# Two changes to a one-core MoE + LoRA kernel: VectorE's rows without a loop, and a later place for an adding transfer

## The reference, cut to what matters

```python
# x (8, 512, 256), cond_8 (8, 8); all float32
rw = softmax(cond_8); w, sel = top_k(rw, 2); w = w / w.sum(-1)      # two experts per batch row
mlp(x, g, u, d) = (gelu(x @ g) * (x @ u)) @ d                        # 256 -> 1024 -> 256
y  = x + mlp(x, shared) + sum over the two experts e of w[b, e] * mlp(x, skill e)
lora(y) = sum over e of cond_8[b, e] * (y @ As[e].T) @ Bs[e].T
out = y + y @ W_base.T + b_base + 2 * lora(y)
```

## Time and profile before

| | |
|---|---|
| runs | 799.68, 799.92, 800.48 us; median 799.92 |
| profiled execution | 800.2 us, of which the span from the first to the last instruction is 798.5 us |
| PE | 790.7 us busy (99%), 4277 matmuls, granted clock 1.000 |
| DVE | 653.6 us busy (82%), 874 instructions |
| ACT | 497.6 us busy (62%) |
| POOL | 311.5 us busy (39%) |
| HBM | 83.53 MB read, 24.64 MB written |

### The profile page before, as it was taken

How to read it: one execution, slowest core, us unless ns; L and a number is a source line. 1 busy time by engine, 2 the same in 40 slices (tenths; PEclk the granted TensorE clock), 3 DMA queues, 4 the chain that set the end, 5 groups by cost and what they waited for, 6 DMA issues and landing times.

```text
span 798.5 us, 14174 instructions
## 1 busy us (share of the span) xinstructions
PE 790.7 (99%) x4277; PEld 687.0 (86%) x4277; DVE 653.6 (82%) x874; ACT 497.6 (62%) x808; POOL 311.5 (39%) x308
## 2 busy tenths in 40 slices
PE   9999999999999999999999999999999999999998
PEld 7888888888888888889889888888998888898897
DVE  4866888888887788878978987888898789789787
ACT  5654564564664576766767666576675667666663
POOL 1531321321430355355344542634634443553441
PEclk9999999999999999999999999999999999999999
DMA  7426506304726742682664465277346526723400
GB/s 202 128 75 197 146 1 195 123 0 145 232 71 185 251 106 77 207 191 81 209 162 110 127 222 123 78 236 173 103 146 206 122 79 219 175 79 107 117 14 28
DMA packets 139894, 108.82 MB, mean 136 GB/s; under 512 B 63040, under 2 KB 131392, under 8 KB 139840
## 3 DMA queue, kind: packets, MB, share of 16 engines
q1 hardware_dynamic: 138688, 104.00, 43.4%
q0 software_dynamic: 1152, 4.19, 3.3%
HBM read 83.53 MB, written 24.64 MB: 135 GB/s over the span
## 4 chain that ended last, share of the span: by engine, by line
PE 89%; issue 4%; POOL 4%; DVE 1%; ACT 1%; POOLq 0%; DVEq 0%; ACTq 0%
PE ps_ring L859 55%; PE ps_acc L859 32%; POOL post L819 1%; POOL stage L805 1%; POOL stage L810 1%; POOL stage L808 1%; POOL stage L806 1%; DVE xc L1589 0%; PE ps_ring L981 0%; PE ps_acc L1075 0%; PE ps_acc L975 0%; DVE wide L1589 0%; PE ps_ring L880 0%; PE ps_ring L885 0%; PE ps_ring L889 0%
## 5 line engine op out<-in xcount | busy, mean ns | idle before, releaser
L859 PE MATMUL ps_ring<-xc,wide 128*128 128x512 f32 (+1 forms) x1854 | 385.6, 356 | 0.0
L859 PEld LDWEIGHTS ps_ring<-xc,wide 128*128 128x128 f32 x1854 | 317.0, 189 | 53.0 <-DVE post L1651 1.0
L1204 ACT CAST inner_hi<-post 128x512 fp32r<-128x512 f32 x192 | 116.2, 621 | 97.6 <-DVE post L1988 32.3
L859 PE MATMUL ps_acc<-inner_hi,wide 128*128 128x512 f32 x504 | 166.4, 390 | 0.0
L1589 DVE TENSOR_TENSOR inner_lo<-post,inner_hi 128x512 fp32r<-128x512 f32 (+1 forms) x145 | 136.4, 950 | 4.0 <-ACT inner_hi L1204 3.7
L1207 ACT ACTIVATE post<-post 128x256 f32<-128x256 f32 (+1 forms) x114 | 62.2, 558 | 99.9 <-DVE post L1912 70.6
L819 POOL TENSOR_TENSOR post<-post 128x256 f32<-128x256 f32 x78 | 82.0, 1071 | 91.4 <-ACT post L1456 91.4
L859 PEld LDWEIGHTS ps_acc<-inner_hi,wide 128*128 128x128 f32 x504 | 94.8, 188 | 18.9
L859 PE MATMUL ps_acc<-inner_lo,wide 128*128 128x512 f32 x252 | 98.5, 391 | 0.0
L859 PE MATMUL ps_acc<-inner_hi,sh_dn 128*128 128x512 f32 x256 | 83.9, 389 | 0.0
L740 POOL TENSOR_TENSOR post<-post 128x512 f32<-128x512 f32 x24 | 31.0, 1293 | 127.3 <-DVE post L1653 127.3
(11 more groups left out here) (127 smaller groups left out, 1067.5 us busy)
## 6 DMA issues: line engine op xcount, KB each, us to landing
rights_scratch<-xc SPq DMA_DIRECT2D x6, 1792.0 KB, 10.2
raw<-n_L_cond_skill_gate_dram SPq DMA_DIRECT2D x32, 256.0 KB, 3.0
raw<-in_L_cond_skill_up_dram SPq DMA_DIRECT2D x32, 256.0 KB, 3.6
raw<-n_L_cond_skill_down_dram SPq DMA_DIRECT2D x32, 256.0 KB, 3.9
xbuf<-n_L_cond_skill_gate_dram SPq DMA_DIRECT2D x32, 256.0 KB, 2.9
xbuf<-in_L_cond_skill_up_dram SPq DMA_DIRECT2D x32, 256.0 KB, 3.4
xbuf<-n_L_cond_skill_down_dram SPq DMA_DIRECT2D x32, 256.0 KB, 3.6
xt_scratch<-xbuf SPq DMA_DIRECT2D x8, 512.0 KB, 3.3
```

Source lines behind the costliest of these rows:

```text
L859: last = pe.matmul(dst, left_[a], right_[b], start=start and n == 0, stop=stop and n == len(PASSES) - 1, skip_group_check=adds)
L1204: return nc.scalar.copy(dst, src)
```

## The change

1. DVE's rows 1 to 7 are called one after another from a Python loop, so the instructions of each are written out and there is no jump; all waits of DVE have constants.
2. On POOL, `add_tokens(b)` moves from behind `ex_c22(b, 1)` to behind `ex_c22(b, 3)` in all rows but the last.
3. In `acc1_to_stage` and `layer1_constants` three waits are dropped, and two pairs of operations on halves become one operation each.

```diff
@@ POOL's row
                 sums_of_weights(b, 2)
                 ex_c22(b, 1)
-                add_tokens(b)
+                if last:
+                    add_tokens(b)
                 sums_of_weights(b, 3)
                 sums_of_weights(b, 4)
                 ex_c22(b, 2)
                 ex_c22(b, 3)
                 if not last:
+                    add_tokens(b)
                     sums_of_weights(b + 1, 0)
                 ex_c22(b, 4)
@@ DVE
             def acc1_to_stage(q):
-                if q > 0:
-                    dve.wait_ge(acc0_out, 2 * q)
                 dve.wait_ge(sh_down_done, 2 * PAIRS * (q + 1))
...
             def layer1_constants():
-
-                dve.wait_ge(acc0_out, 2 * Q)
-                dve.wait_ge(layer1_landed, 6 * 16)
                 dve.wait_ge(a_hi, 1)
-                for half in (slice(0, P), slice(P, H)):
-                    last = take_lo(a_s[1][:, half], a_nat[:, half], a_s[0][:, half])
-                last.then_inc(a_ready, 1)
+                take_lo(a_s[1], a_nat, a_s[0]).then_inc(a_ready, 1)
                 dve.wait_ge(turned_w, 1)
                 V.tensor_copy(b_t[:], ps_misc[1][:, 0:H]).then_inc(b_t_done, 1)
-                for c in range(HC):
-                    last = V.tensor_copy(w_id[:, c * H:(c + 1) * H], ps_misc[0][:, c * H:(c + 1) * H])
-                last.then_inc(w_turned, 1)
+                V.tensor_copy(w_id[:], ps_misc[0][:]).then_inc(w_turned, 1)
...
-            def row(b, par, first, last, steps=range(K)):
+            def row(b, par, first, last):
...
-                for k in steps:
+                for k in range(K):
...
             row(0, 0, True, False)
-            row(1, 1, False, False, range(DVE_TURN_STEP))
-            with dve.Fori(0, (B - 2) // 2) as i:
-                row(i * 2 + 1, 1, False, False, range(DVE_TURN_STEP, K))
-                row(i * 2 + 2, 0, False, False)
-                row(i * 2 + 3, 1, False, False, range(DVE_TURN_STEP))
-            row(B - 1, 1, False, True, range(DVE_TURN_STEP, K))
+            for b in range(1, B):
+                row(b, b % 2, False, b == B - 1)
             dve.wait_ge(base_ready, B * 16)
```

More of the change, by code:

```diff
@@ L64, in cond_resid_kernel @@
     TURN_STEP = 6
-    DVE_TURN_STEP = 8
     SEVEN = [1, 3, 5, 6, 7]
```

## The result

The changed kernel takes 804.97 us (median of 6 runs, 804.46 to 807.30) against 799.80 us before: 1.0067 times as long, 95% interval 1.0054 to 1.008. It is slower where 795.5 us was forecast. The profiled execution was 805.2 us with a span of 803.5.

The account below looks back on a forecast made before the run. PE was taken as the bound, busy 790.7 of 798.5 us, losing time in rows 3 and 5 to DVE's jumps. From the 799.92 us median, 4.44 less (2.49 + 1.95), other terms 0, gave 795.48, forecast 795.5; range 795.0 to 798.0.

Parts of the forecast that it names:

- DVE's loop goes: Rows 3 and 5: without DVE's jumps back both fall to 66.84 us, gaining 2.49 + 1.95 = 4.44 us.
- Both rivals on late code: DVE's written-out rows: one unhidden fetch, 797.97 us, chance 0.07; or one in every row, 812.9 us, chance 0.03.
- the stall that stays: Rows 3 and 5: pause not from DVE's jump, or another engine's jump replaces it; time stays 799.9 us, chance 0.04.
- Constants and waits: Row 0 on DVE: merged operations save at most 0.9 us, which becomes idleness, and dropped waits were long met: 0.
- The adding transfer moves: POOL, behind C22 of step 12: the 0.86 us issue fits within 2.62 us of waiting before step 14's C22: 0.
- The rival of the slower side: POOL, rows 0 to 6: issue outgrows its 2.62 us cover, delaying C22 of step 14; 801.6 us at 3.5, chance 0.02.
- the 5% for slower: Chance of a slower kernel: late code in every row, 0.03, plus the issue outgrowing its cover on POOL, 0.02.

Follow-up runs that it names:

- e1_written_out: The changed kernel with the adding transfer put back in its old place behind ex_c22(b, 1), DVE's rows still written out: 794.90 us, ratio 0.9936.
- e2_move_only: The kernel before with only the adding transfer's move, DVE's loop kept: 808.11 us, ratio 1.0102.
- e3: e1_written_out plus a 16-column adding transfer into a spare tile, in the new place, row 0 only: 796.77 us in one execution.
- e4: e1_written_out with 8 already-met semaphore waits on POOL, no transfer, ahead of its additions for the next row: 794.91 us, ratio 0.9936.
- e9: e1_written_out with 16 already-met semaphore waits on POOL, no transfer, ahead of its additions for the next row: 795.19 us, ratio 0.9942.
- e5: e1_written_out with one more POOL addition of 320 columns where the changed kernel issues the transfer, no transfer there: 795.12 us, ratio 0.9941.
- e12: The changed kernel with 13 already-met semaphore waits on POOL between the transfer's issue and the additions behind it: 796.99 us, ratio 0.9968.
- e11: The changed kernel with POOL's second addition behind the transfer's issue made to wait until the first is written: 795.74 us, ratio 0.9943.

## Why the prediction was wrong

- *DVE's loop goes*: right, mechanism and size. In e1_written_out rows 3 and 5 are at 66.84, which is the 4.44 us; ACT's and the other engines' jumps cost nothing, and the changed kernel shows no DVE pause marked "issue" above 0.5 us. Both rivals on late code fall, and so does the stall that stays. Its 794.90 us, against 795.48 worked out, are 4.90 under the 799.80 of before and 5.37 under the 800.27 measured beside it. The surplus lies ahead of row 0, which began some 0.7 us earlier than in the profile of before; in the other runs' profiles, e2_move_only with DVE's loop kept among them, it began 0.3 to 0.8 us earlier, so the loop isn't the cause.
- *Constants and waits*: nothing to be seen, as forecast.
- *The adding transfer moves*: this is the step that failed. It put the move at 0 where it costs 9.8 us. All that was checked there held: the issue took 0.87 us, C22 of step 14 waited for ACT even longer (3.76 us), and the tokens were in time. But the step asked only what waits for POOL by a semaphore. It did not ask what runs beside POOL without one. The row it quoted, a POOL operation stretched from 0.74 to 1.93 us beside DVE, was the sign that the two engines hold each other up; it was read as a cost to POOL alone, with DVE as the one that never waits. In the place where the transfer went, POOL's sums already ran beside DVE's multiplication of step 12, on the chain gelu, multiplication, ACT's high part, ACT's copy, PE. It was delayed by 2.35 - 0.71 = 1.64 us, and PE lost 1.35 of that.
- *The rival of the slower side* on the transfer named the wrong victim, C22 of step 14, and the wrong price: it needed an issue of over 3.25 us, and one of 0.87 us was enough. Its 2% was far too low, and so was all of the 5% for slower: the whole chance on that side had been given to mechanisms with a semaphore or a fetch in them.

The cause as far as it is shown: with an adding transfer issued on POOL directly ahead of a run of POOL additions, the issue shown to overlap the first of them by 0.22 us or more, a DVE multiplication with both operands in SBUF is held until the run has a gap. The amount of data doesn't matter (e3), nor the time of the sums (e4, e9), nor a run as such (e5), nor the issue alone (its old place), nor that the issue has only just ended (e12); a gap ends the hold (e11). Not tried: a transfer from POOL that doesn't add. Whether the overlap is what does it or only goes with it (the distance of the starts fits too), why it persists through the additions, and why DVE isn't let in between them then, stays open.

The Trainium skill, page "SBUF — State Buffer", section "SBUF: two separate sides", says that DVE and GpSimd share one pair of ports as an exclusive lock, that a DVE instruction with two SBUF inputs takes part in it only against a GpSimd operation that reads SBUF, and that whichever starts first has the pair for its whole instruction while the other is blocked. The runs agree with the block, and with the PSUM-fed addition not being held. They go beyond the rule in its length: DVE waited here (2.35 us) not for the one instruction that was running, but for three.

## What to carry to other kernels

Before a POOL instruction is moved, read the DVE instructions that will run beside it and beside what it pushes later, not only what waits for POOL; a DVE instruction with both operands in SBUF on the critical chain is what to look for. Put an adding transfer issued by POOL ahead of an idle stretch of POOL, not ahead of a run of its additions: in this kernel the old place and the one behind sums 0 both cost nothing, and e1_written_out, the written-out rows with the transfer in its old place, is as fast as any version measured, at 794.90 us. When two edits come together, a net result hides both: here 4.4 us gained and 9.8 lost.

## What the runs showed of the hardware that was not expected

- In the rows shown the multiplication, where it meets the sums, ends 0.27 to 0.29 us after the end of a POOL addition: of the first or second where successive POOL instructions overlap by 0.10 us or less, or where a gap follows (e11), and of the third where they overlap by about a third of a microsecond.
- POOL's additions start 0.70 us apart in both cases; behind an overlapping issue only their shown length grows, from 0.74 to 1.02 us.
- The issue of an adding transfer of 16 columns takes POOL as long as one of 1024 mostly does: 0.87 us. The 1.00 us of the full one in row 0 is that of the first such issue of the kernel; in e3_tiny the small one came second in row 0.
- Waits that are already met, behind an issue: 8 moved the next addition by some 0.05 us, 13 by 0.25, 24 by 0.73.
